# Attention with softmax on one core: one head pair in eight scored once and turned by a transfer, with the weighted sums a pair later

## The reference

```python
q = einsum('bnd,hde->bhne', layernorm(x), Wq) / sqrt(64)      # 16 heads of 64
k, v = the same with Wk, Wv
attn = softmax(einsum('bhne,bhme->bhnm', q, k), axis=-1)
x = x + concat_heads(einsum('bhnm,bhme->bnhe', attn, v)) @ Wp + bp
x = x + FFN(layernorm(x))      # 128 -> 512, gelu, layernorm, 512 -> 128, ternary weights
```

## Time and profile before

| | us |
|---|---|
| median of 3 runs (lowest, highest) | 993.33 (992.51, 994.14) |
| the profiled execution, its own time | 994.11 |
| its span, first to last instruction | 992.3 |
| TensorE matmul busy / weight loads busy | 970.0 / 769.5 |
| DVE / ACT / POOL busy | 852.3 / 733.4 / 864.0 |

### The profile page before, as it was taken

One profiled execution on the slowest core, in us unless ns is written; L12 is line 12 of the kernel. 1 busy time (PEld: TensorE's weight loads), 2 busy tenths in 40 slices (PEclk: granted clock), 3 DMA queues, 4 the chain that ended last, 5 costly groups with the idle time before them and its releaser, 6 DMA issues.

```text
span 992.3 us, 39211 instructions
## 1 busy us (share of the span) xinstructions
PE 970.0 (98%) x15932; PEld 769.5 (78%) x15932; DVE 852.3 (86%) x1742; ACT 733.4 (74%) x1180; POOL 864.0 (87%) x850
## 2 busy tenths in 40 slices
PE   7899999999999999999999999999999999989998
PEld 6577777877777887877888887777788787767776
DVE  5998988888888988998888988998889888758877
ACT  4787777787777777777777777877777778677775
POOL 5789898989886999999999999999999999988885
PEclk8999999999999999999999999999999999999999
DMA  6112223342223343223333223233333333467976
GB/s 135 43 31 53 47 54 71 63 63 63 68 48 57 63 82 66 49 57 63 84 64 58 63 72 50 58 64 83 64 63 64 63 63 64 79 124 156 178 165 129
DMA packets 242786, 74.08 MB, mean 75 GB/s; under 512 B 218032, under 2 KB 240304, under 8 KB 242608
## 3 DMA queue, kind: packets, MB, share of 16 engines
q1 hardware_dynamic: 240528, 71.05, 36.7%
q10 hardware_dynamic: 2080, 0.52, 0.3%
HBM read 11.41 MB, written 8.39 MB: 20 GB/s over the span
## 4 chain that ended last, share of the span: by engine, by line
PE 92%; DVE 2%; ACT 2%; DMA 2%; issue 1%; POOL 1%; SPq 0%; DVEq 0%; ACTq 0%
PE S L765 11%; PE PV L790 8%; PE M L725 7%; PE PV L792 6%; PE PV L791 6%; PE QK L713 5%; PE QK L714 5%; PE QK L712 5%; PE misc L765 5%; PE S L757 5%; PE M L843 2%; PE M L808 2%; PE M L844 2%; PE M L845 2%; PE misc L757 2%; PE M L810 2%
## 5 line engine op out<-in xcount | busy, mean ns | idle before, releaser
L1325 POOL TENSOR_TENSOR pl<-p 128x1024 f16<-128x1024 f32 x254 | 478.6, 1896 | 33.0 <-ACT p L1102 32.7
L1526 DVE TENSOR_REDUCE negmax<-M 128x4 f32<-128x1024 f32 x252 | 306.6, 1217 | 22.3 <-PE M L725 16.2
L1110 ACT ACTIVATE QKh<-QK 128x512 f16<-128x512 f32 x251 | 149.5, 596 | 143.5 <-PE QK L714 142.8
L1102 ACT ACTIVATE p<-S,s_exp 128x1024 f32<-128x1024 f32 x173 | 192.1, 1111 | 56.9 <-PE S L765 56.3
L790 PEld LDWEIGHTS PV<-V,p 128*128 128x128 bf16 x2048 | 186.6, 98 | 45.5 <-issue 34.7
L790 PE MATMUL PV<-V,p 128*128 128x65 f16 x2048 | 214.8, 193 | 2.8 <-DVE O L1540 2.0
L791 PE MATMUL PV<-V,p 128*128 128x64 f16 x2048 | 213.2, 192 | 0.0
L792 PE MATMUL PV<-V,pl 128*128 128x65 f16 x2048 | 212.5, 194 | 0.0
L1546 DVE TENSOR_TENSOR QKl<-QK,QKh 128x512 f16<-128x512 f32 x251 | 172.2, 686 | 43.5 <-ACT QKh L1110 42.4
L791 PEld LDWEIGHTS PV<-V,p 128*128 128x128 bf16 x2048 | 189.0, 97 | 4.7
L792 PEld LDWEIGHTS PV<-V,pl 128*128 128x128 f16 x2048 | 188.7, 97 | 0.0
(11 more groups left out here) (246 smaller groups left out, 2474.4 us busy)
## 6 DMA issues: line engine op xcount, KB each, us to landing
y_kept<-yTb SPq DMA_DIRECT2D x32, 128.0 KB, 1.7
yT<-y_kept SPq DMA_DIRECT2D x16, 256.0 KB, 3.4
result<-X SPq DMA_DIRECT2D x15, 256.0 KB, 3.0
X<-in_L_attn_query SPq DMA_DIRECT2D x7, 512.0 KB, 4.3
OT<-O SPq DMA_TRANSPOSE x64, 4.0
shift<-negmax SPq DMA_TRANSPOSE x63, 2.3
O<-in_L_attn_Wk ACTq DMA_DIRECT2D x2, 256.0 KB, 5.1
O<-in_L_attn_Wq SPq DMA_DIRECT2D x2, 256.0 KB, 5.7
```

The source lines that it names most:

```text
L1102: e.activation(p32[r][:, :, :, :].rearrange("p i m n -> p (i m n)"), score_bank(p)[:, :], ACT.Exp, scale=s_exp[:, :]).then_inc(s_ex, 1)
L1325: e.tensor_tensor(pl[r][:, :, :, :].rearrange("p i m n -> p (i m n)"), p32[r][:, :, :, :].rearrange("p i m n -> p (i m n)"), p_high(r).rea ...
L1526: e.tensor_reduce(dst[:, :, NB * jj:NB * jj + NB], max_bank(p)[:, :].rearrange("p (i t m) -> p i t m", i=2, t=NB), AX.X, ALU.max, negate=T ...
```

## The change

Of every batch from pair 87 on, the last pair (j = 7; 87, 95, ... 239, 20 pairs) becomes **direct**. It has no `max_scores` and no turned shift. `direct_scores` makes its exact scores once, with queries on the partitions, in `misc`; DVE's `direct_max` takes the row maxima from them; ACT turns these into a bias of four columns (`bias_rows`), and runs four exps of 256 columns with that bias. ACT copies the high half into rows (`p_rows`, in the memory of the later `a` buffers), POOL writes the low half beside it, and SP turns both with one DMA transpose, from which the weighted sum reads its stationary side (`p_parts`, in `p_turned`).

In a pass with a direct pair (j = 6) the max scores of pair t + 7 are held back; the next pass (j = 0) makes them, and drops those of its own t + 7, which is the next direct pair (`held_back`, `two_maxima`). Each pass keeps two maxima on DVE, the direct one among them.

The weighted sums of the section are W(t - 3) and W(t - 2) in place of W(t - 2) and W(t - 1), with their division on DVE. The extra W at step 79 goes, and step 240 gets one. Counts of semaphores are adapted (`maxima_to`, `direct_no`).

```diff
+DIRECT_0, DIRECT_1 = 87, 240
...
+def direct(p):
+
+    return p % HP == HP - 1 and DIRECT_0 <= p < DIRECT_1
+
+
+def direct_no(p):
+
+    return sum(direct(k) for k in range(p))
+
+
+def maxima_to(p):
+
+    return p + 1 - direct_no(p + 1)
+
+
+def held_back(t):
+
+    return t % 4 == 2 and TWO_0 <= t and direct(t + MAX_LEAD + 3)
+
+
+def two_maxima(t):
+
+    first = [t + MAX_LEAD - 1] if held_back(t - 2) else []
+    last = [] if held_back(t) or direct(t + MAX_LEAD + 1) else [t + MAX_LEAD + 1]
+    return first + [t + MAX_LEAD] + last
...
-    return t - PV_LAG if 0 <= t - PV_LAG < NP and t != TWO_1 else None
+    return t - PV_LAG if 0 <= t - PV_LAG < NP else None
...
+        a_all = sb("a_all", [P, A_RING, F])
+        a = [a_all[:, i, :] for i in range(A_RING)]
+        p_rows = a_all[:, 2:4, :].rearrange("p a f -> p (a f)").bitcast(F16).rearrange("p (s c) -> p s c", s=2)
+        p_turned = a_all[:, 0:2, :].rearrange("p a f -> p (a f)").bitcast(F16)
+        neg_rows, bias_rows = sb("neg_rows", [P, 2, NB]), sb("bias_rows", [P, 2, NB])
...
+            def turn_p(p):
+                d = direct_no(p)
+                e.wait_ge(s_dhi, d + 1)
+                e.wait_ge(s_dlo, d + 1)
+                if d:
+                    e.wait_ge(s_pv, p - HP + 1)
+                e.dma_start_transpose(p_turned.rearrange("p (c n) -> p c n", n=P),
+                                      p_rows.rearrange("p s c -> p (s c)")).then_inc(p_in_turned, 16)
...
+            def direct_scores(p):
+                h, lo = QKh[p % QK_RING], QKl[p % QK_RING]
+                e.wait_ge(s_qklo, p + 1)
+                e.wait_ge(s_ex, p - 1)
+                for t in range(NB):
+                    tok = slice(t * P, (t + 1) * P)
+                    for n, (q, k) in enumerate(((h, h), (lo, h), (h, lo))):
+                        for i in range(2):
+                            rows = head_rows(i)
+                            op = e.matmul(misc_pair[:, i * 512 + t * N:i * 512 + (t + 1) * N], q[rows, 0, tok], k[rows, 1, :],
+                                          start=n == 0, stop=n == 2, skip_group_check=True)
+                            if t == NB - 1 and n == 2:
+                                op.then_inc(s_sc, 1)
...
-                max_scores(t + MAX_LEAD)
+                max_scores(two_maxima(t)[0])
                 scores(t)
-                scores(t + 1)
-                max_scores(t + 1 + MAX_LEAD)
-                weighted(t - 2)
+                if direct(t + 1):
+                    direct_scores(t + 1)
+                else:
+                    scores(t + 1)
+                for p in two_maxima(t)[1:]:
+                    max_scores(p)
+                weighted(t - 3)
                 queries_keys(t + Q_LEAD + 1)
                 for piece in two_values(t):
                     values(*piece)
                 if two_project(t):
                     project_tile(*two_project(t), t)
-                weighted(t - 1)
+                weighted(t - 2)
...
+            def direct_exps(p):
+                r, d = p % P_RING, direct_no(p)
+                e.wait_ge(s_dmx, d + 1)
+                e.activation(bias_rows[:, :, :], neg_rows[:, :, :], ACT.Identity, scale=s_exp[:, :]).then_inc(s_dbias, 1)
+                e.wait_ge(s_dbias, d + 1)
+                e.wait_ge(s_pv, p - P_RING + 1)
+                for i in range(2):
+                    for t in range(NB):
+                        op = e.activation(p32[r][:, i, t, :], misc_pair[:, i * 512 + t * N:i * 512 + (t + 1) * N], ACT.Exp,
+                                          scale=s_exp[:, :], bias=bias_rows[:, i, t:t + 1])
+                op.then_inc(s_ex, 1)
+
+            def direct_high(p):
+                d = direct_no(p)
+                e.wait_ge(s_ex, p + 1)
+                if d:
+                    e.wait_ge(p_in_turned, 16 * d)
+                e.activation(p_rows[:, 0, :].bitcast(BF16), p_high(p % P_RING).rearrange("p i m n -> p (i m n)"),
+                             ACT.Copy).then_inc(s_dhi, 1)
...
                 exps(t)
-                exps(t + 1)
+                if not direct(t + 1):
+                    exps(t + 1)
                 qk_high(t + Q_LEAD + 1)
+                if direct(t + 1):
+                    direct_exps(t + 1)
...
+                    direct_high(t + 1)
...
+            def direct_low(p):
+                r, d = p % P_RING, direct_no(p)
+                e.wait_ge(s_ex, p + 1)
+                if d:
+                    e.wait_ge(p_in_turned, 16 * d)
+                e.tensor_tensor(p_rows[:, 1, :], p32[r][:, :, :, :].rearrange("p i m n -> p (i m n)"),
+                                p_high(r).rearrange("p i m n -> p (i m n)"), ALU.subtract).then_inc(s_dlo, 1)
...
+            def direct_max(p):
+                d = direct_no(p)
+                e.wait_ge(s_sc, 2 * p + 2)
+                if d:
+                    e.wait_ge(s_dbias, d)
+                e.tensor_reduce(neg_rows[:, :, :], misc_pair[:, :].rearrange("p (i t m) -> p i t m", i=2, t=NB),
+                                AX.X, ALU.max, negate=True).then_inc(s_dmx, 1)
...
+                max_out(two_maxima(t)[0])
                 qk_low(t + MAX_LEAD + 1)
-                max_out(t + MAX_LEAD + 1)
-                sums_inverse(t - 2)
-                normalise(t - 2)
+                if direct(t + 1):
+                    direct_max(t + 1)
+                for p in two_maxima(t)[1:]:
+                    max_out(p)
+                sums_inverse(t - 3)
+                normalise(t - 3)
                 qk_low(t + Q_LEAD + 1)
                 for piece in two_values(t):
                     v_low(*piece)
```

More of the change, by code:

```diff
@@ L149, in low_on_pool_before @@
 def low_on_pool_before(p):
-    return p - sum(d < p for d in LOW_ON_DVE)
+    return p - sum(d < p for d in LOW_ON_DVE) - direct_no(p)
 def shift_group(t):
@@ L384, in layer @@
         yT = [sb(f"yT{i}", [P, FG, 2, P], F16) for i in range(Y_RING)]
-        a = [sb(f"a{i}", [P, F]) for i in range(A_RING)]
+        a_all = sb("a_all", [P, A_RING, F])
[3 more added lines that the diff above has]
+        neg_rows, bias_rows = sb("neg_rows", [P, 2, NB]), sb("bias_rows", [P, 2, NB])
         zTh = [sb(f"zTh{i}", [P, FC, P], BF16) for i in range(3)]
@@ L419, in layer @@
         s_sc, s_ex, s_pl, s_pl_dve = sem("s_scores"), sem("s_exp_done"), sem("s_p_lo"), sem("s_p_lo_dve")
+        s_dmx, s_dbias, s_dhi, s_dlo, p_in_turned = (
+            sem(f"s_direct_{n}") for n in ("max", "bias", "p_hi", "p_lo", "p_transposed"))
         s_pv, s_rs, s_o = sem("s_pv"), sem("s_rsum"), sem("s_o")
@@ L645, in sp_program @@
                         turn_shift(shift_group(t))
+                    if t and direct(t - 1):
+                        turn_p(t - 1)
                     if x_split_batch(*divmod(t - 1, HP)) is not None:
@@ L720, in max_scores @@
                 if p >= 2:
-                    e.wait_ge(s_mx, p if p >= FIRST else p - 1)
+                    e.wait_ge(s_mx, maxima_to(p - 1) if p >= FIRST else p - 1)
                 for t in range(NB):
@@ L747, in scores @@
                 elif p == PAIRED:
-                    e.wait_ge(s_mx, NP)
+                    e.wait_ge(s_mx, maxima_to(NP - 1))
                 elif p > PAIRED:
@@ L768, in scores, with p_parts @@
                                 op.then_inc(s_sc, 1)
+            def direct_scores(p):
[11 more added lines that the diff above has]
+                                op.then_inc(s_sc, 1)
+            def p_parts(p, i, m, t):
+                if direct(p):
+                    parts = p_turned.rearrange("p (s i t m n) -> p s i t m n", s=2, i=2, t=NB, m=NB)
+                    return parts[:, 0, i, t, m, :].bitcast(BF16), parts[:, 1, i, t, m, :]
+                tok = slice(t * P, (t + 1) * P)
+                return p_high(p % P_RING)[:, i, m, tok], pl[p % P_RING][:, i, m, tok]
             def weighted(p):
                 b, j = divmod(p, HP)
-                r = p % P_RING
-                ph = p_high(r)
-                if p in LOW_ON_DVE:
+                if direct(p):
+                    e.wait_ge(p_in_turned, 16 * (direct_no(p) + 1))
+                elif p in LOW_ON_DVE:
                     e.wait_ge(s_pl_dve, LOW_ON_DVE.index(p) + 1)
@@ L789, in weighted @@
                             v = V[b % 2][:, m, 2 * j + i, :]
-                            e.matmul(PV[:, c0:c0 + E + 1], ph[:, i, m, tok], v[:, E:2 * E + 1], start=m == 0, stop=False)
-                            e.matmul(PV[:, c0:c0 + E], ph[:, i, m, tok], v[:, 0:E], start=False, stop=False)
-                            op = e.matmul(PV[:, c0:c0 + E + 1], pl[r][:, i, m, tok], v[:, E:2 * E + 1],
+                            hi, lo = p_parts(p, i, m, t)
+                            e.matmul(PV[:, c0:c0 + E + 1], hi, v[:, E:2 * E + 1], start=m == 0, stop=False)
+                            e.matmul(PV[:, c0:c0 + E], hi, v[:, 0:E], start=False, stop=False)
```

(33 more changed lines are left out.)

1 line of the change is left out of this document (removed).

## The result

The changed kernel takes 997.69 us (median of 5 runs, 996.18 to 998.77) against 992.85 (5 runs, 991.72 to 994.14): ratio 1.0045, 95% interval 1.0033 to 1.0058. It is slower, by 4.8 us. The profiled execution took 997.69 us with a span of 995.9.

The account below looks back on a forecast made before the run. TensorE, busy 98% of the span and 92% of the chain, was taken as the bound. Removed work - 8.8 and the weighted-sum wait + 14.8 gave + 6.0 us on the median 993.33: 999.3 us, range 996 to 1006.

Parts of the forecast that it names:

- Work removed: TensorE, pass j = 6: no max-score or shift matmuls for 20 direct pairs, 0.44 us each, 8.8 us less.
- The wait for the weighted sum: Passes j = 0 and 4: odd pair's exp waits for W(t - 3), next pass 0.37 us later, 40 times, 14.8 us more.
- the chain has no air behind 518.83: Pass with values: from QKh's start through QKl and `v_low` to the next pass, nothing absorbs a delay; full 0.37 us added.
- Passes with a projection: Passes j = 2 and 6: QKl ends at 5.57 us, TensorE wants its bank at 5.95; no cost, 0.38 us of cover.
- The direct pair beside TensorE: From pass j = 6: ACT's bias, four exps and copy to rows stay covered, thinly; cost 0, range 0 to 4 us.
- rival 3: The direct pair comes late as well, on ACT or for POOL: 0.3 to 0.6 us a batch, say 1008; chance 0.13.
- The transfer: DMA transpose of the direct pair lands in 4.0 us, at 12.7; its weighted sum comes at 15.5, cover 2.8 us.
- A wait for the transposed pair: Sign of being wrong: TensorE waits for the transposed pair in the changed trace.
- The ends of the section: At both ends of pairs 80 to 239, sums only shift by one pass: no cost.
- the value chain hides the wait: Rival 1: TensorE's own work, not `v_low`, closes the pass, so only - 8.8 stays: 984.5 us; chance 0.08.
- POOL is the bound: Rival 2: POOL's unchanged work holds the pass, taking away both gain and loss: 993.3 us; chance 0.04.

Follow-up runs that it names:

- five buffers: The changed kernel with P_RING = 5 in place of 4: 986.96 us, ratio 0.9939 to the kernel before.
- doubled copy: The changed kernel with a second 1024-column copy on ACT for each direct pair, into a buffer that nothing reads: 1012.52 us, ratio 1.019 to the kernel before.

## Why the prediction was right

The forecast was 999.3 us, 6.0 over the median shown; measured are 997.69, and 4.8 over the kernel before. Sign and mechanism hold; the sizes of its terms:

- **Work removed: right.** 0.44 us a direct pair was forecast. The direct pass fell from 6.61 to 6.14, 0.47; a batch with five buffers is 25.87 against 26.34 without direct pairs (314.0 to 827.7).
- **The wait for the weighted sum: right, but 0.07 us too large.** Forecast 0.37 us in each of 40 passes, measured 6.86 and 6.87 against 6.57, 0.30. It came of two parts that partly cancel. The weighted sum reached ACT more slowly than DVE's 0.04 (its end at 518.58, exp at 518.66, 3.28 us into the pass and not 3.22), and QKh began 4.30 us in, not 4.24. But "the chain has no air behind 518.83" was wrong: in the kernel before, the value copies and not QKl came last. The second copy and the second `v_low` before, then after:

```profile
520.14 0.60 ACT L1119 ACTIVATE V<-M 128x512 f16<-128x512 f32 x1
520.78 0.69 DVE L1552 TENSOR_TENSOR V<-M,V 128x512 f16<-128x512 f32 x1
```

```profile
520.64 0.61 ACT L1209 ACTIVATE V<-M 128x512 f16<-128x512 f32 x1
521.50 0.68 DVE L1666 TENSOR_TENSOR V<-M,V 128x512 f16<-128x512 f32 x1
```

  Before, TensorE's value matmuls end at 520.11, the copy follows at 520.14 and `v_low` starts 0.03 us behind the copy's end; so it is for both `v_low` in all 39 passes with values from 316 to 836 us. After, `v_low` starts 0.15 and 0.26 us behind its copy, held by DVE's own queue. So from QKl's start to the last `v_low`'s end it takes 1.89 us (520.30 to 522.19) where it took 2.01 (519.46 to 521.47), and QKh had 0.12 us of air that the delay used up first. I had said that DVE's side is the later one and carried over the whole old distance. By the experiments the wait costs 10.7 to 11.9 us, not 14.8.
- **Passes with a projection: right.** j = 2 stays at 6.61, though exp idles longest there for its weighted sum (0.84 us, until 525.53, in the pass that starts at 522.24). QKl ends 5.62 us in and TensorE wants its bank 5.95 us in, where 5.57 and 5.95 were forecast. So how long exp idles says nothing of what its wait costs.
- **The direct pair beside TensorE: right, with more cover.** A bias takes 0.29 us (0.3 taken), the four exps 1.94 (2.2 taken), the copy 1.07 (1.03). The exps end 6.21 us into their pass instead of 6.4, and the cover before the odd exp is 0.39 us instead of 0.05. The doubled copy shows that the cover ends there: rival 3 had the right place, but needed the even exp to end 9.7 us in, and it ended at 9.16.
- **The transfer: right, with less to spare than forecast.** It was issued at 517.59 and lands in 4.6 us (median of 20), not 4.0; the weighted sum that reads it waited once, 0.2 us. A wait for the transposed pair was named as a sign of being wrong; this one is too small to count. But with five buffers it came twice, up to 1.0 us (1.3 in all), so the cover of 2.8 us is at times used up.
- **The ends of the section: wrong, but small.** I put nothing there. In the last direct pass (t = 238) the max scores of t + 7 aren't held back, since no direct pair follows that would give them a place. So DVE has three reductions in it, and the projection, which wants M, waits:

```profile
827.34 1.22 DVE L1632 TENSOR_REDUCE negmax<-M 128x4 f32<-128x1024 f32 x1
...
829.08 1.22 DVE L1640 TENSOR_REDUCE neg_rows<-misc 128x4 f32<-128x1024 f32 x1
830.21 1.22 DVE L1632 TENSOR_REDUCE negmax<-M 128x4 f32<-128x1024 f32 x1
...
831.48 0.23 PE L910 MATMUL M<-Wph,OT 128*128 128x128 f16 x1 [0.88 <-DVE negmax L1632]
```

The third reduction ends at 831.43, and the projection's first matmul, idle for 0.88 us, starts at 831.48: 0.9 us once.

In sum, in the section: 40 x 0.30 - 20 x 0.47 + 0.9 = 3.5 us, where 6.0 was forecast; the residual's span gained 3.2, the whole 3.6 in the profiled runs and 4.8 in the medians. That the medians lie nearer to the forecast than the terms do is luck: the difference between the medians and the profiled runs, about a microsecond, lies within what executions of one kernel differ by (994.4 to 996.9 us of span for this one).

**The rivals.** That the value chain hides the wait is out: with the wait removed the time falls by 1.1%. It had a grain of truth, the 0.12 us above: TensorE's own values, through their copy and `v_low`, did close the pass before. That POOL is the bound is out: POOL's work is the same and five buffers bring the kernel to 987. Taking matmuls away did give something, though POOL with its 87% would come first by the rule of the Trainium skill, "Perfetto Trace Analysis", Identifying the Most-Contended Engine. The runs don't bear that rule out here as the prediction applied it, with the share of weight loads; that section of the Trainium skill names MFU (the share of peak arithmetic) beside it, which is not worked out here.

## What to carry to other kernels

A consumer that comes later holds its buffer longer. Before moving it, look up who waits for that buffer, and above all what is queued behind the waiting instruction on its engine: here the exp itself was in no hurry, but QKh and, through it, QKl and the bank M were. Then the cure is one more buffer, if memory allows, or to place the waiting instruction behind the urgent ones, and then to look again at what has slid behind it. And when a change frees a busy engine and the time grows, compare the chains: the share that the busy engine lost names the engines of the new chain.

## What the runs showed of the hardware

DVE's QKl and the two `v_low` took 1.89 us from first start to last end when each value copy had ended before its `v_low` was due, and 2.01 when each `v_low` followed its copy, though the work is the same (0.68 to 0.69 us an instruction). With its input there, the second `v_low` starts 0.09 us before the first one ends (521.50 against 521.59); behind its copy it started 0.04 before (520.78 against 520.82). These 0.12 us were as large as a third of the effect forecast for each pass. An exp of 256 columns with a bias from memory starts every 0.46 us or so (four in 1.94 us), against 1.02 for 1024 columns in one: the four pieces cost ACT 0.8 us more than the whole.
